# Cross-attention and quantised feed-forward: the opening in another order

## The chip, the cores and the metric

The kernel runs on one core of one Trainium2 chip. The metric is the device time of one execution in microseconds (us); the kernel before has a median of 1361.93 us over 3 runs (1360.26 to 1363.41). The engines are TensorE (PE, whose weight loads the profile counts apart as PEld), VectorE (DVE), ScalarE (ACT), GpSimd (POOL) and SyncE (SP), which here issues all the DMAs.

## The reference

The input `x` is 8 x 1024 rows of 512; the context has 8 x 64 rows of 512. There are 16 heads of 64.

```python
lat = layernorm(_layernorm(x), ln_l_w, ln_l_b); c = layernorm(ctx, ln_c_w, ln_c_b)
q = lat @ Wq;  k, v = split(c @ Wkv)
attn = softmax(clip(q @ k.T * 64**-0.5, -11, 11))        # per head
x = x + (attn @ v) @ Wo + bo
xq = fake_quant(_layernorm(x), clip_x)                   # one scale for the whole tensor
h = fake_quant(silu(xq @ wq8(w_gate).T) * (xq @ wq8(w_up).T), clip_down)
x = x + h @ wq8(w_down).T
```

## The kernel before, in words

The kernel has an opening (0 to 99.4 us), an attention part in 16 groups of 512 rows, and a feed-forward part. The change touches the opening alone.

The attention never forms the queries. For each batch entry the keys are folded with the query weights into a matrix M (tile `M`), so that the scores of a group are products of the normalised rows with M; the values are folded with the output weights in the same way (`value_fold`, `VW`). All of these products run as three float16 matmuls on high and low halves (`split_products`, L78 to L80). So every operand is made twice: ScalarE writes the high half, VectorE the low half (`weight_high` L492 and `weight_low` L713, `kv_high` L497 and `kv_low` L718, `q_high` L503 and `q_low` L722, `wo_high` L508 and `wo_low` L727, and for M `fold_key` L420 and L605).

The opening goes through these stages, each engine in the order in which its program is written:

1. Loads: context, vectors, then query weights (`wq32`, in the place of `x`), key weights (`wk32`, in the place of `M`), value weights (`wv32`, in the place of `E`), two groups of `x`. ScalarE sums the squares of each weight matrix (`square`, L485), from which its scale follows through a small matmul (`weight_sum` L1053 or `spread_rows` L1057) and a chain of small VectorE operations.
2. Key products: the first two together, chunk by chunk (`first_products`), then six more (`product(0, n)`, 12 matmuls each). Behind each, four transposes of query weights (`turn_q`, L1115).
3. Value products (`product(1, n)`, eight times 12 matmuls). Among them stand the folding of M (`fold_keys`, L991, 48 small matmuls for each quarter), the score bias (`project_bias` L1092, eight columns; `split_q_bias` L778 to L784; `bias_product` L1101, 24 matmuls; `bias_expand` L1107) and the first rows of group 0 (`norm_rows`, `high_y`, `low_y`, and the DMA transpose `turn`).
4. Step 0: eight tiles of scores of group 0 (`score`, tile `ring`), each followed on ScalarE by `cap` L445, `floor` L451 and `exp` L455, while the rows of group 1 are normalised; then `fold_values` (L1015), the denominators, and step 1.

An engine runs strictly in the order of its program. Engines meet by semaphores: PE starts a product only when `kv_low` has freed one of the two banks `po`, a quarter of the fold only when `m_lo` says that VectorE has taken the quarter before the last, and the first score when `m_lo` has reached 8. The identifiers `wk_lo`, `wv_lo`, `c_lo`, `squared2`, `m_lo` in the rows of the order are such semaphores.

## Time and profile before

| | us |
|---|---|
| median of 3 runs | 1361.93 |
| profiled execution | 1363.62 |
| its span in the trace | 1361.9 |
| PE busy (95% of the span) | 1289.0 |
| DVE busy | 1166.1 |
| ACT busy | 787.2 |

The span is what the trace covers; the profiled execution's own time is 1.7 us longer. All places are given in us from the start of the span. "Idle before" in a row of a timeline is the time in which the engine stood still just before, and the arrow names who released it. In the lines of the kernel before, the chain of waits is on PE for nearly all of the time.

### The profile page before, as it was taken

What the parts mean: (1) busy time and instruction counts of PE and PEld (TensorE: products, weight loads), DVE (VectorE), ACT (ScalarE), POOL (GpSimd) and SP (SyncE); (2) the same over time, 40 slices, a digit from 0 to 9 for tenths busy, and PEclk for the clock granted to TensorE, in tenths of its full rate; (3) what the DMA queues carried; (4) which work ended last, traced back from release to release, by engine and by line L of the source; (5) the groups of instructions that cost most, each with busy time, mean ns of one, the idle gap of its engine ahead of it and who ended that gap; (6) DMA issues with size and microseconds to landing.
All of it is one profiled execution on the core that took longest, in us unless ns stands there. A gap on an engine that the chain in (4) does not pass through costs nothing.

```text
span 1361.9 us, 20412 instructions
## 1 busy us (share of the span) xinstructions
PE 1289.0 (95%) x7625; PEld 610.7 (45%) x7668; DVE 1166.1 (86%) x2059; ACT 787.2 (58%) x1183; POOL 409.0 (30%) x278
## 2 busy tenths in 40 slices
PE   7988999999999999999999999699999999799997
PEld 6433444544544445445444444344444444344343
DVE  6757899988988998889889857789999999789996
ACT  6557765776577557755764762233443443597671
POOL 2104424542454244424443521000000000045555
PEclk9998999999999999999999999899999999899999
DMA  7173525446246245362561335296666632299995
GB/s 286 43 220 105 128 81 158 135 124 202 74 127 216 64 148 163 109 205 59 155 219 54 115 125 131 101 284 218 204 253 254 252 104 63 93 391 423 424 400 189
DMA packets 179218, 241.72 MB, mean 177 GB/s; under 512 B 121632, under 2 KB 140848, under 8 KB 168112
## 3 DMA queue, kind: packets, MB, share of 16 engines
q1 hardware_dynamic: 179120, 240.43, 53.2%
q8 instruction: 60, 0.98, 0.3%
q14 instruction: 38, 0.31, 0.1%
HBM read 120.86 MB, written 90.57 MB: 155 GB/s over the span
## 4 chain that ended last, share of the span: by engine, by line
PE 71%; DVE 14%; ACT 5%; issue 4%; SPq 3%; DMA 2%; POOL 1%; POOLq 0%; DVEq 0%; ACTq 0%
PE pu L1482 10%; PE pg L1476 10%; PE pu L1510 7%; PE po L78 7%; PE po L80 7%; PE po L79 7%; PE ring L79 6%; PE ring L78 6%; PE ring L80 6%; DVE w L1448 2%; PE ring L1015 1%; ACT E L451 1%; DVE sg L1455 1%; PE ring L991 1%; SPq L1247 1%
## 5 line engine op out<-in xcount | busy, mean ns | idle before, releaser
L1351 ACT ACTIVATE sg<-pg,gate_scale 128x512 f32<-128x512 f32 x176 | 120.9, 687 | 186.9 <-PE pg L1476 186.9
L78 PE MATMUL ring<-yT,M 128*128 128x512 f16 x512 | 195.5, 382 | 0.0
L80 PE MATMUL ring<-yT,M 128*128 128x512 f16 x512 | 195.4, 382 | 0.0
L79 PE MATMUL ring<-yT,M 128*128 128x512 f16 x512 | 195.4, 382 | 0.0
L78 PE MATMUL po<-VW,p 128*128 128x512 f16 x480 | 182.8, 381 | 2.0 <-DVE p L633 2.0
L1476 PE MATMUL pg<-xqT,w 128*128 128x512 bf16 x689 | 179.5, 380 | 3.7 <-DMA xqT<-xq 2.0
L80 PE MATMUL po<-VW,p 128*128 128x512 f16 x480 | 182.7, 381 | 0.0
L79 PE MATMUL po<-VW,p 128*128 128x512 f16 x480 | 182.5, 380 | 0.0
L1482 PE MATMUL pu<-xqT,w 128*128 128x512 bf16 x690 | 179.7, 380 | 0.7
L1510 PE MATMUL pu<-w 128*128 128x512 bf16 x690 | 157.4, 386 | 19.6 <-DVE w L1450 10.1
L392 POOL TENSOR_TENSOR esum<-esum,E 128x512 f32<-128x512 f32 x96 | 131.0, 1365 | 76.3 <-ACT E L455 76.2
L633 DVE TENSOR_TENSOR p<-E,p 128x512 f16<-128x512 f32 x120 | 143.9, 1200 | 6.5 <-ACT p L466 6.5
L466 ACT ACTIVATE p<-E 128x512 f16<-128x512 f32 x120 | 75.0, 625 | 126.4 <-DVE E L629 124.3
L1410 DVE TENSOR_TENSOR hb<-pu,sg 128x512 f32<-128x512 f32 x176 | 120.5, 685 | 30.9 <-PE pu L1482 29.4
L1368 ACT ACTIVATE hb<-hb,magic,hscale 128x512 f32<-128x512 f32 x176 | 125.2, 801 | 31.0 <-DMA hb<-hidden 27.2
L1414 DVE TENSOR_REDUCE hmax_g<-hb 128x1 f32<-128x512 f32 x176 | 117.4, 674 | 0.0
L1510 PEld LDWEIGHTS pu<-w 128*128 128x128 bf16 x704 | 68.4, 99 | 108.3 <-DVE sg L1455 14.5
L383 POOL TENSOR_TENSOR x<-x,bo 128x512 f32<-128x512 f32 x64 | 100.5, 1571 | 33.1 <-DVE y L597 33.1
L601 DVE TENSOR_TENSOR y<-y 128x512 f16<-128x512 f32 x64 | 56.3, 879 | 61.9 <-ACT y L416 61.8
L1476 PEld LDWEIGHTS pg<-xqT,w 128*128 128x128 bf16 x704 | 68.9, 98 | 86.8 <-DMA xqT<-xq 2.5
L1482 PEld LDWEIGHTS pu<-xqT,w 128*128 128x128 bf16 x704 | 69.1, 98 | 83.7 <-issue 1.1
L1336 POOL PARTITION_ALL_REDUCE one<-one x2 | 0.7, 350 | 348.2 <-DVE one L1435 316.8
(239 smaller groups left out, 2152.4 us busy)
## 6 DMA issues: line engine op xcount, KB each, us to landing
hidden<-hb SPq DMA_DIRECT2D x11, 2816.0 KB, 9.7
hb<-hidden SPq DMA_DIRECT2D x11, 2816.0 KB, 18.4
xa<-x_rows_d SPq DMA_DIRECT2D x28, 1024.0 KB, 6.1
x<-in_x_dram SPq DMA_DIRECT2D x16, 1024.0 KB, 5.8
value_fold<-E SPq DMA_DIRECT2D x64, 256.0 KB, 2.5
VW<-value_fold SPq DMA_DIRECT2D x16, 1024.0 KB, 6.1
x_rows_d<-x SPq DMA_DIRECT2D x16, 1024.0 KB, 4.9
out_dram<-xa SPq DMA_DIRECT2D x12, 1024.0 KB, 12.7
```

The lines of the kernel that those rows point to most:

```text
L78: nc.tensor.matmul(out, a_hi, b_hi, start=first, stop=False)
L79: nc.tensor.matmul(out, a_hi, b_lo, start=False, stop=False)
L80: return nc.tensor.matmul(out, a_lo, b_hi, start=False, stop=last)
L392: nc.gpsimd.tensor_tensor(esum[:], esum[:], E[:, g % 2, t], ALU.add).then_inc(sums, 1)
L633: nc.vector.tensor_tensor(probs(g, 1, t), E[:, g % 2, t], probs(g, 0, t), ALU.subtract).then_inc(prob_lo, 1)
L1351: nc.scalar.activation(sg[:, n % 4], pg[n % 4][:], ACT.Silu, scale=gate_scale[:, n % FT:n % FT + 1]).then_inc(silus, 1)
L1368: nc.scalar.activation(hb[:, slot, m], hb[:, slot, m], ACT.Identity, scale=hscale[:, m:m + 1], bias=magic[:, 0:1]).then_inc(h_scaled, 1)
L1410: nc.vector.tensor_tensor(hb[:, HOME[g], i], pu[n % 4][:], sg[:, n % 4], ALU.mult).then_inc(hs, 1)
L1414: nc.vector.tensor_reduce(hmax_g[:, i:i + 1], hb[:, HOME[g], i], AX.X, ALU.max, apply_absolute_value=True).then_inc(reaches, 1)
L1476: ins = nc.tensor.matmul(pg[n % 4][:], wg[:, c, at], xqT[:, g % 2, c], start=(c == 0), stop=(c == DC - 1))
L1482: ins = nc.tensor.matmul(pu[n % 4][:], wu[:, c, at], xqT[:, g % 2, c], start=(c == 0), stop=(c == DC - 1))
L1510: ins = nc.tensor.matmul(pu[t][:], hq[:, q % 2, m, t * P:(t + 1) * P], wd[:, m], start=(m == 0), stop=(m == FT - 1))
```

## The change

The loads of the opening come in the order keys, queries, values. The output weights are loaded into the place of `M` instead of `E`, as soon as the key weights have been converted. The four transposing DMAs of group 0 are issued ahead of the store of the keys. The eight `project_bias` columns leave the stretch before the key products and stand behind `product(0, 2)` to `product(0, 7)` and behind the first two value products. The squares of two chunks of query weights and of the value weights are taken later. The folding of M is done in one piece in front of the last value product. The output weights get their halves beside value products 3 to 6, where `norm_stats(1)` stands as well, and the score bias is finished at value product 4.

```diff
@@ -128,7 +128,8 @@
     wide = lambda half: half.rearrange("p (c n) -> p c n", c=DC)
     wk32 = wide(M[:, :, :, :, :].rearrange("p a c t u -> p (a c t u)").bitcast(fp32))
     wq32 = wide(x[:, 2:4].rearrange("p g t d -> p (g t d)"))
-    wv32, wo32 = wide(E[:, 1].rearrange("p t n -> p (t n)")), E[:, 1]
+    wv32 = wide(E[:, 1].rearrange("p t n -> p (t n)"))
+    wo32 = M[:, :, :, :, :].rearrange("p a c t u -> p (a c t u)").bitcast(fp32).rearrange("p (k n) -> p k n", k=IC)
     halves16 = lambda flat: flat.rearrange("p (a c n) -> p a c n", a=2, c=DC)
     parts16 = lambda flat: flat.rearrange("p (b a c s) -> p b a c s", b=NB, a=2, c=IC)
     vw_flat = VW[:, :, :, :].rearrange("p a t n -> p (a t n)")
@@ -256,9 +257,9 @@
             wkv_of = wkv.rearrange("(c p) (k n) -> k p c n", p=P, k=2)
             wq_of = wq.rearrange("(c p) n -> p c n", p=P)
             for c in range(DC):
+                sp.dma_start(wk32[:, c], wkv_of[0][:, c]).then_inc(ld_w[0][c], 16)
+            for c in range(DC):
                 sp.dma_start(wq32[:, c], wq_of[:, c]).then_inc(ld_w[1][c], 16)
-            for c in range(DC):
-                sp.dma_start(wk32[:, c], wkv_of[0][:, c]).then_inc(ld_w[0][c], 16)
             for c in range(DC):
                 sp.dma_start(wv32[:, c], wkv_of[1][:, c]).then_inc(ld_w[2][c], 16)
             load_x(0)
@@ -319,13 +320,14 @@
             sp.dma_start(x1_d[g], x[:, g % 4]).then_inc(x1_stored[g % 4], 16)
 
         load_opening()
-        sp.wait_ge(w_lo[1], DC)
+        sp.wait_ge(w_lo[0], DC)
         for c in range(DC):
             sp.dma_start(wo32[:, 2 * c:2 * c + 2], wo.rearrange("(c p) n -> p c n", p=P)[:, 2 * c:2 * c + 2]).then_inc(ld_w[3][c], 16)
-        store_kv(0)
         for t in range(TT):
             turn(0, t)
+        store_kv(0)
         sp.wait_ge(q_lo, IC)
+        sp.wait_ge(qb_ready, 1)
         for g in range(2, 4):
             load_x(g)
         sp.wait_ge(kv_stored, 16)
@@ -417,6 +419,8 @@
 
         def fold_key(b, u):
             act.wait_ge(m_psum, 8 * b + u + 1)
+            if b == 0 and u == 0:
+                act.wait_ge(o_lo, DC)
             nc.scalar.activation(M2[:, 0, u // 2, :, u % 2, :], ring[u % 4][:].rearrange("p (t u) -> p t u", t=KT),
                                  ACT.Copy, scale=mcol[:, u // 2:u // 2 + 1]).then_inc(m_hi, 1)
 
@@ -510,41 +514,44 @@
         act.wait_ge(magic_set, 2)
         nc.scalar.activation(warm[:], magic[:, 0:1], ACT.Identity)
         for c in range(DC):
+            square(0, wk32[:, c], c)
+        for c in range(2):
             square(1, wq32[:, c], c)
-        for c in range(DC):
-            square(0, wk32[:, c], c)
         act.wait_ge(scales, 1)
         for c in range(DC):
             act.wait_ge(c_turned, c + 1)
             nc.scalar.activation(cT[:, 0, c, :], ring[c][:], ACT.Identity, scale=ccol[:, 0, c:c + 1], bias=ccol[:, 1, c:c + 1]).then_inc(c_hi, 1)
             nc.scalar.activation(cf[:, c], ring[c][:], ACT.Identity, scale=ccol[:, 0, c:c + 1], bias=ccol[:, 1, c:c + 1]).then_inc(c_full, 1)
-            if c > 0:
-                weight_high(0, c - 1)
-        weight_high(0, DC - 1)
-        square(2, wv32[:, 0], 0)
+            weight_high(0, c)
         kv_high(0, 0)
         kv_high(0, 1)
-        for n in range(IC):
-            if n >= 2:
-                kv_high(0, n)
+        square(1, wq32[:, 2], 2)
+        square(1, wq32[:, 3], 3)
+        square(2, wv32[:, 0], 0)
+        for n in range(2, IC):
+            kv_high(0, n)
+            q_high(n - 2)
+            if n < 5:
+                square(2, wv32[:, n - 1], n - 1)
+            if n >= 6:
+                weight_high(1, n - 6)
+        for n in range(6, IC):
             q_high(n)
-            if n < 3:
-                square(2, wv32[:, n + 1], n + 1)
-            if n >= 4:
-                weight_high(1, n - 4)
+            weight_high(1, n - 4)
         act.wait_ge(ld_misc, 48)
         nc.scalar.activation(keep.clips[:], keep.clips[:], ACT.Exp, scale=-1.0).then_inc(sig, 1)
         for n in range(IC):
+            if n == IC - 1:
+                for u in range(KT):
+                    fold_key(0, u)
             kv_high(1, n)
             if n < 4:
-                fold_key(0, 2 * n)
-                fold_key(0, 2 * n + 1)
                 high_y(0, n)
-            if n in (3, 4):
-                for c in range(2 * n - 6, 2 * n - 4):
+            if n < 2:
+                for c in range(2 * n, 2 * n + 2):
                     square(3, wo32[:, 2 * c:2 * c + 2].rearrange("p k n -> p (k n)"), c)
-        for k in range(DC):
-            wo_high(k)
+            if 3 <= n < 7:
+                wo_high(n - 3)
 
         for s in range(NG):
             more = s + 1 < NG
@@ -814,54 +821,59 @@
         context_centre()
         vectors_known()
         scale_by_sum(WK, po[1][:, 0:DC], 1, 2)
-        rows_seen(WQ, 0)
         for c in range(DC):
             dve.wait_ge(c_full, c + 1)
             nc.vector.tensor_tensor(cT[:, 1, c, :], cf[:, c], cT[:, 0, c, :], ALU.subtract).then_inc(c_lo, 1)
-            if c > 0:
-                weight_low(0, c - 1)
-        weight_low(0, DC - 1)
-        scale_by_rows(WQ, misc[:, 0:P], 2, 3)
-        norm_stats(0)
+            weight_low(0, c)
         kv_low(0, 0)
         kv_low(0, 1)
+        rows_seen(WQ, 0)
+        norm_stats(0)
+        kv_low(0, 2)
+        scale_by_rows(WQ, misc[:, 0:P], 2, 3)
         q_low(0)
-        q_low(1)
-        for n in range(2, IC):
+        for n in range(3, IC):
             kv_low(0, n)
+            q_low(n - 2)
+            if n == 3:
+                norm_aggregates(0)
+            if n == 4:
+                norm_rstd(0)
+            if n == 5:
+                scale_by_sum(WV, misc[:, 0:DC], 2, 4)
+            if n >= 6:
+                weight_low(1, n - 6)
+        for n in range(6, IC):
             q_low(n)
-            if n == 2:
-                norm_aggregates(0)
-                norm_rstd(0)
-            if n == 3:
-                scale_by_sum(WV, misc[:, 0:DC], 2, 4)
-            if n >= 4:
-                weight_low(1, n - 4)
+            weight_low(1, n - 4)
         norm_rows(0, 0)
         norm_rows(0, 1)
-        split_q_bias()
         score_scales()
         for n in range(IC):
+            if n == IC - 1:
+                for u in range(KT):
+                    fold_key(0, u)
             kv_low(1, n)
             if n < 4:
-                fold_key(0, 2 * n)
-                fold_key(0, 2 * n + 1)
                 low_y(0, n)
                 if n < 2:
                     norm_rows(0, n + 2)
-            if n == 5:
+            if n == 1:
+                split_q_bias()
                 rows_seen(WO, 1)
-            if n == 6:
+            if n == 2:
                 scale_by_rows(WO, pd[:, 0:P], 3, 5)
-            if n == 7:
+            if n == 3:
                 dve.wait_ge(bias_rows, 1)
                 nc.vector.tensor_copy(bias_rows_sb, misc[0:H, :]).then_inc(rows_out, 1)
-        score_biases()
-        norm_stats(1)
+            if n == 4:
+                score_biases()
+            if 3 <= n < 7:
+                wo_low(n - 3)
+            if n == 6:
+                norm_stats(1)
         norm_aggregates(1)
         norm_rstd(1)
-        for k in range(DC):
-            wo_low(k)
 
         for s in range(NG):
             more = s + 1 < NG
@@ -1071,8 +1083,6 @@
                     ins = product_chunk(0, n, c)
                     if c == DC - 1:
                         ins.then_inc(kv_ready[0], 1)
-                if c < 2:
-                    project_bias(6 + c)
 
         def product(kind, n):
 
@@ -1120,10 +1130,6 @@
         pe.wait_ge(ld_vec, 64)
         nc.tensor.transpose(misc[:, 0:4 * DC], vec_rows, keep.ident32[0:4 * DC, 0:4 * DC]).then_inc(const_turned, 1)
         spread_vectors()
-        for c in range(DC):
-            pe.wait_ge(ld_w[1][c], 16)
-        project_bias(0)
-        project_bias(1)
         for t in range(TT):
             pe.wait_ge(c_centred, t + 1)
             for c in range(DC):
@@ -1131,28 +1137,35 @@
                 if t == TT - 1:
                     ins.then_inc(c_turned, 1)
         weight_sum(0, po[1][:, 0:DC])
-        project_bias(2)
-        spread_rows(0, misc[:, 0:P], 2)
-        for n in range(3, 6):
-            project_bias(n)
         first_products()
+        for c in range(DC):
+            pe.wait_ge(ld_w[1][c], 16)
         turn_q(0)
         turn_q(1)
         for n in range(2, IC):
             product(0, n)
+            if n == 2:
+                spread_rows(0, misc[:, 0:P], 2)
             turn_q(n)
-            if n == 3:
+            project_bias(n - 2)
+            if n == 4:
                 pe.wait_ge(scales, 3)
                 weight_sum(2, misc[:, 0:DC])
         for n in range(IC):
+            if n == IC - 1:
+                for c in range(DC):
+                    fold_keys(0, c)
             product(1, n)
-            if n < 4:
-                fold_keys(0, n)
-            if n == 6:
+            if n < 2:
+                project_bias(n + 6)
+            if n == 2:
                 pe.wait_ge(qb_split, 2)
                 spread_rows(1, pd[:, 0:P], 3)
+            if n == 3:
+                pe.wait_ge(scales, 4)
                 bias_product()
-        bias_expand()
+            if n == 4:
+                bias_expand()
 
         for s in range(NG):
             more = s + 1 < NG
```

Three places show what moves. The first is PE from the end of the context's transposes (`weight_sum`, into `po`) to the second chunk of the first key products. Before:

```order
L1053 MATMUL po<-weight_squares,ones_row 128x4 [waits squared0]
L1092 MATMUL pd<-vector_cols,x 128x1 x4
L1057 MATMUL misc<-ffn_raw,ones_row 128x128 [waits spread_in]
L1092 MATMUL pd<-vector_cols,x 128x1 x12
L78 MATMUL po<-cT,VW 128x512 [waits wk_lo,wk_hi,c_lo]
L79 MATMUL po<-cT,VW 128x512
L80 MATMUL po<-cT,VW 128x512
L78 MATMUL po<-cT,VW 128x512
```

and after the change:

```order
L1065 MATMUL po<-weight_squares,ones_row 128x4 [waits squared0]
L78 MATMUL po<-cT,VW 128x512 [waits wk_lo,wk_hi,c_lo]
L79 MATMUL po<-cT,VW 128x512
L80 MATMUL po<-cT,VW 128x512
L78 MATMUL po<-cT,VW 128x512
L79 MATMUL po<-cT,VW 128x512
```

The sixteen `project_bias` matmuls of these rows (into `pd`) and the spread of the query weights' scale that stood in front are gone; of the eight columns none is left here.

The second is ACT at the end of the key products: L497 and L501 are `kv_high`, L503 and L507 `q_high`, L492 and L496 `weight_high` of the value weights. Before, from `product(0, 6)` on:

```order
L497 ACTIVATE p<-po 128x8x64 [waits k_ready]
L503 ACTIVATE w<-ring,operand_scales 128x512 [waits q_turned]
L492 ACTIVATE E<-E,operand_scales 128x1024
L497 ACTIVATE p<-po 128x8x64 [waits k_ready]
L503 ACTIVATE w<-ring,operand_scales 128x512 [waits q_turned]
L492 ACTIVATE E<-E,operand_scales 128x1024
L536 ACTIVATE clips<-clips 128x2 [waits ld_misc]
```

and after the change, from `product(0, 7)` on:

```order
L501 ACTIVATE p<-po 128x8x64 [waits k_ready]
L507 ACTIVATE w<-ring,operand_scales 128x512 [waits q_turned]
L496 ACTIVATE E<-E,operand_scales 128x1024
L507 ACTIVATE w<-ring,operand_scales 128x512 [waits q_turned]
L496 ACTIVATE E<-E,operand_scales 128x1024
L507 ACTIVATE w<-ring,operand_scales 128x512 [waits q_turned]
L496 ACTIVATE E<-E,operand_scales 128x1024
L542 ACTIVATE clips<-clips 128x2 [waits ld_misc]
```

Behind the last key product one query piece and one value chunk stood before; now there are three query pieces and three value chunks.

The third is DVE at the folding of M (L605 and L612 are the low halves of `fold_key`). Before, with the rows of group 0 (`y`) between them:

```order
L718 TENSOR_TENSOR VW<-po,VW 128x8x64 [waits v_hi16,open_step]
L605 SCALAR_TENSOR_TENSOR M<-ring,key_cols,M 128x8x64 [waits m_hi] x2
L601 TENSOR_TENSOR y<-y 128x512 [waits y_hi]
L597 TENSOR_SCALAR y<-x,mv,rs 128x512 [waits y_lo]
L718 TENSOR_TENSOR VW<-po,VW 128x8x64 [waits v_hi16]
L605 SCALAR_TENSOR_TENSOR M<-ring,key_cols,M 128x8x64 [waits m_hi] x2
```

and after the change, where L734 is `wo_low`, L585 `norm_stats(1)` and L725 `kv_low`:

```order
L725 TENSOR_TENSOR VW<-po,VW 128x8x64 [waits v_hi16]
L734 SCALAR_TENSOR_TENSOR w<-M,operand_scales,w 128x1024 [waits wo_hi]
L585 BN_STATS st<-x 128x6 [waits x_loaded1]
L585 BN_STATS st<-x 128x6 x3
L612 SCALAR_TENSOR_TENSOR M<-ring,key_cols,M 128x8x64 [waits m_hi] x8
L725 TENSOR_TENSOR VW<-po,VW 128x8x64 [waits v_hi16]
L591 BN_AGGR mv<-st 128x2 [waits ln_step] x4
```

The eight low halves of M now stand in one row, behind the last piece of output weights and the statistics of group 1.

## Rows read from the trace of the kernel before

**Rows 1.** Page, busy time of the engines over the span

```profile
PE 1289.0 (95%) x7625; PEld 610.7 (45%) x7668; DVE 1166.1 (86%) x2059; ACT 787.2 (58%) x1183; POOL 409.0 (30%) x278
```

**Rows 2.** Timeline of PE: start, us, engine, line, xcount [idle before <-releaser]

```profile
22.17 5.12 PE L1092 MATMUL pd<-vector_cols,x 128*128 128x1 f32 x24
...
39.73 1.04 PE L1115 MATMUL ring<-ident,x 128*128 128x128 f32 x8
...
58.54 0.60 PE L1115 MATMUL ring<-ident,x 128*128 128x128 f32 x4
...
62.41 0.38 PE L78 MATMUL po<-yT,E 128*128 128x512 f16 x1 [3.27 <-DVE E L713]
```

**Rows 3.** Timeline of PE, value products to the first score

```profile
66.78 0.87 PE L991 MATMUL ring<-p,w 64*128 64x64 f16 x48
...
88.26 5.35 PE L1101 MATMUL misc<-p,ffn_raw 128*16 128x512 f16 x24
...
98.37 1.12 PE L1107 MATMUL misc<-rexp,head_rows 16*128 16x512 f32 x2 [2.07 <-DVE rexp L858]
...
99.43 0.39 PE L78 MATMUL ring<-yT,M 128*128 128x512 f16 x1
```

**Rows 4.** Timeline of ACT and PE in step 0

```profile
100.53 0.63 PE L80 MATMUL ring<-yT,M 128*128 128x512 f16 x1
...
111.87 0.63 ACT L416 ACTIVATE y<-y 128x512 f16<-128x512 f32 x1 [3.83 <-DVE y L597]
...
127.58 0.71 ACT L455 ACTIVATE E<-E,score_bounds 128x512 f32<-128x512 f32 x1
...
134.57 0.59 PE L78 MATMUL ring<-yT,M 128*128 128x512 f16 x1
```

**Rows 5.** Chain of waits, start, us, what: single matmuls and one turn

```profile
32.67 0.43 PE po L78
...
43.43 0.44 PE ring L1115 x4
...
44.51 0.22 PE po L78
```

**Rows 6.** Timeline up to the first key products, DVE, ACT and POOL

```profile
17.93 0.23 DVE L754 TENSOR_SCALAR context_cols<-vector_cols,operand_scales 128x8 f32<-128x8 f32 x1
...
19.04 0.78 ACT L519 ACTIVATE cT<-ring,context_cols 128x512 f16<-128x512 f32 x1 [0.36 <-PE ring L1130]
...
26.43 2.21 ACT L492 ACTIVATE VW<-M,operand_scales 128x1024 f16<-128x1024 f32 x2
...
27.36 10.18 POOL L397 COPY yT<-cT 128x512 f16<-128x512 f16 x8 [24.43 <-DVE cT L820]
...
27.64 3.88 DVE L713 SCALAR_TENSOR_TENSOR VW<-M,operand_scales,VW 128x1024 f16<-128x1024 f32 x2 [0.35 <-ACT VW L492]
```

**Rows 7.** Timeline of ACT and DVE, end of the key products

```profile
44.71 1.07 ACT L485 ACTIVATE E<-E 128x1024 f16<-128x1024 f32 x1
...
58.74 0.60 ACT L497 ACTIVATE p<-po 128x512 f16<-128x512 f32 x1 [0.82 <-PE po L80]
...
60.98 1.28 DVE L713 SCALAR_TENSOR_TENSOR E<-E,operand_scales 128x1024 f16<-128x1024 f32 x1 [0.26 <-ACT E L492]
```

**Rows 8.** Timeline of ACT and DVE: operations that the change moves

```profile
63.09 0.21 DVE L778 TENSOR_SCALAR scale_tmp<-operand_scales 128x1 f32<-128x1 f32 x1
...
66.04 0.16 DVE L788 TENSOR_TENSOR scale_tmp<-operand_scales 128x1 f32<-128x1 f32 x1
...
74.69 1.26 ACT L420 ACTIVATE M<-ring,key_cols 128x512 f16<-128x512 f32 x2 [0.21 <-PE ring L991]
...
75.41 1.41 DVE L605 SCALAR_TENSOR_TENSOR M<-ring,key_cols,M 128x512 f16<-128x512 f32 x2 [0.20 <-ACT M L420]
...
101.15 2.47 DVE L578 BATCH_NORM_STATS2 st<-x 128x6 f32<-128x512 f32 x4
...
106.51 4.87 DVE L727 SCALAR_TENSOR_TENSOR w<-E,operand_scales,w 128x1024 f16<-128x1024 f32 x4
```

## Prediction

> **What bounds the kernel now.** I read the page first, for the share of TensorE: it is busy 1289.0 of 1361.9 us [rows 1], so what the change can move is time in which PE stands still or runs slowly. The change touches the opening alone, so I then read the waits of PE up to 140 us, the chain of waits there, and the timelines of the three engines. The reader is to see four stretches, each ending with an instruction of PE that exists before and after:
>
> A: start to the end of the first pair of key products, 39.73 us.
> B: from there to the first value product, 62.41: 22.68 us. It ends with a wait of 3.27 us for the last low half of the value weights [rows 2].
> C: to the first score, 99.43: 37.02 us. Its last wait is 2.07 us in front of `bias_expand` [rows 3].
> D: step 0, to the first score of step 1, 134.57: 35.14 us [rows 3, 4].
>
> What follows is the same work in the same order, so I let any shift at 134.57 stand in the total.
>
> In A PE runs at half rate: matmuls of 512 columns follow each other by 0.43 us, against 0.22 later; that is 1.2 and 2.4 GHz [rows 5].
>
> **Stretch A: earlier.** Before, twelve `project_bias` matmuls (three columns) hold PE from 22.17 for 5.12 us, so the first key product starts behind them, though its operands are there sooner; two more columns stand between the chunks. All leave. What is late next is the conversion of the key weights. ScalarE starts it at 19.04, when PE has turned the context; VectorE has the scales 18.16 (17.93 + 0.23). With no columns ahead of it, PE turns the context earlier, and with keys loaded first the squares of the keys are done earlier too, so ScalarE starts at about 18.2, 0.8 sooner. Its last high half then ends at 27.8 instead of 28.6 (26.43 + 2.21), and the low half follows at 29.2 to 30.1: the last two took 3.88 us beside GpSimd's copies, 1.94 each, against 1.28 for one alone [rows 6, 7]. Six matmuls remain behind it: 1.3 us at the high level, 2.6 at the low. I take 31.9 (30.5 to 33): A gains 7.8 us, 6.7 to 9.2.
>
> The Trainium skill, "SBUF — State Buffer", section "SBUF: two separate sides", says that VectorE with two SBUF inputs and a GpSimd operation reading SBUF exclude each other for a whole instruction. GpSimd's eight copies took 10.18 us [rows 6], so by that rule the last low half could wait one copy, 1.27, and end at 30.5 instead of 29.9; the trace's 1.94 lies between. By that rule A would gain 0.5 us less.
>
> **Stretch B: longer.** Before, PE needs 18.81 us from 39.73 to the end of `product(0, 7)` at 58.54 [rows 2]. Now comes on top:
> - Five of the eight columns in front of that point. A column costs 5.12 / 3 = 1.7 at the low level. The trace shows none at the high level; the ends are 0 (it hides under other loads) and 1.7. I take half, 0.85, as for the matmuls of [rows 5]: 4.2 us.
> - The spread of the query scale, 0.4, and a wait of about 0.5 for it: ScalarE now squares two chunks of query weights and one of value weights behind `kv_high(0, 1)`, at 1.07 and a read of the sum each [rows 7].
> - `weight_sum(2)` behind `product(0, 4)`. The last square of the value weights now stands behind `kv_high(0, 4)` and `q_high(2)`: 0.6 + 0.6 + 1.2 = 2.4, and ScalarE is a further 1 us behind from the squares before it; PE has 0.44 (four transposes) + 0.85 of other work [rows 5]. Wait 2.0 (0.5 to 2.5). Before, that square came one product earlier and cost nothing.
>
> So 25.9 us to the end of `product(0, 7)`. The first value product then waits for ScalarE, whose row is now one `kv_high`, three `q_high` and three `weight_high` (one, one and one before): 0.60 + 3 x (0.6 + 1.1) = 5.7, and a last low half, 1.28, with 0.1 of hand-over: 7.1 us instead of 3.87 (58.54 to 62.41) [rows 2, 7]. B takes 33.0 us, 10.3 more; ends 30 and 35.
>
> **Stretch C: longer.** Up to the end of value product 6: 84 matmuls at 0.22, 18.5; `bias_product` 5.35; `bias_expand` 1.12, its rows now copied in time; two columns 1.7; the spread of the output scale 0.4 [rows 3, 5]. New is a wait in front of that spread: the last column ends the second product's slot, then VectorE does `kv_low`, `low_y`, `norm_rows` and `split_q_bias` (63.09 to 66.04, 2.95 us) and `rows_seen`, while PE has one product of 2.6: 2.3 us (0 to 3). And the low clock after the wait of 7 us: after 3.27 us of idling it showed low matmuls too; I count 2.5 us (1 to 3.4). Sum 31.9 us.
>
> Then the fold. PE does two quarters and needs VectorE's low halves of the first before the third. On VectorE stand ahead of them `kv_low` 0.6, the last `wo_low` 1.2 and `norm_stats(1)` 2.47; with ScalarE's `kv_high` 0.6 and `wo_high` 1.05 in front of `wo_low`, they start 5.4 us after value product 6. Eight low halves at 0.68 (1.41 for a pair, overlapped) follow, broken by the alternation with PE and ScalarE (0.87 for a quarter, 1.26 for two high halves) [rows 3, 8]. M's first half is free at 5.4 + 1.4 = 6.8, the third quarter ends at 7.7, the fourth at 8.5 to 9.3, and the last value product at 11.7. Before, the quarters stood between products and PE did not wait for them. I add 1.0 for the clock after a wait of 5 us. C: 31.9 + 11.7 + 1.0 = 44.6, 7.6 more; ends 39 and 48. The DMAs that move (output weights earlier, transposes ahead of the store) only end waits of ScalarE that PE never felt; the output weights are asked for 30 us before they are squared, and the first conversion of M waits for `wo_low` at 3 us, inside the 5.4.
>
> **Stretch D: shorter.** Before, the 4.87 us of `wo_low`, the statistics of group 1 and its scale chain stand on VectorE behind the first score; ScalarE waits 3.83 us for rows until 111.87. Now only the scale chain, about 2.8 us, remains, and it runs beside the first tile. The pace is then PE's, 96 matmuls at 0.22 = 21.1, plus 1.5 for the low level (it fell at 100.53 before), then cap, floor, rows and exp of the last tile, 2.8, and from the end of exp (127.58 + 0.71) to step 1 as before, 6.3: 31.7 us, 3.4 less; ends 26 and 33 [rows 4, 8].
>
> **Sum.** -7.8 + 10.3 + 7.6 - 3.4 = +6.7 us on the profiled execution of 1363.62 (span 1361.9 and 1.7 around it): 1370.3. That execution lies 1.7 above the median of 1361.93; the forecast for the median is 1368.6, rounded to 1368.
>
> **Rivals.**
> 1. *Step 0 becomes PE's and the clock holds (faster).* If ScalarE's tile of about 2.4 us stays under PE's 2.6 and the fold of the values runs through, step 0 is 21.1 + 3 for the folds + 1.8 for the denominators = 25.9, 9.2 less instead of 3.4. With the 3.5 us of low clock counted in C gone too: 6.7 - 5.8 - 3.5 = -2.6, and with the wait for the last squares at its low end, -4.1: 1357.8. For it: ScalarE waited for rows in step 0 and no longer does. Against: the 6.3 us behind the last exp are a chain of exp, fold and denominators that the change doesn't touch. It decides from a step 0 under 27 us.
> 2. *The added waits are half as long (no change).* If a column costs little at the high level and VectorE comes to the fold 3 us earlier, B and C lose 6 us less: +0.7, 1362.6. For it: columns were never measured at the high level. Against: the row of seven ScalarE instructions has measured prices.
> 3. *The low level follows each new wait.* The waits of 2 us at `weight_sum(2)` and of 2.3 us at the spread each bring slow matmuls, as the 2.07 us wait did, behind which matmuls took 0.63 from 100.53 on [rows 3, 4]. A stretch like A's shows the price, 0.21 a matmul; 8 to 12 of them at each place: +4, 1372.6. The Trainium skill, "TensorE: Matmul & The Clock Gate", section "HAM oscillation — how this bites in real kernels", says that every wait that makes the array idle long enough starts the next matmuls slowly again. The trace agrees behind 98.37; by that rule this rival is what happens.
>
> **Chances.** Forecast 0.45 (own range 1365 to 1371), rival 3 0.18, rival 2 0.2, rival 1 0.17. A measurement of this kernel can tell about 0.2%, 2.7 us, from no change. Faster 0.17, within it 0.21 and slower 0.62. The range that should hold the time 8 times in 10: from just under rival 2 toward rival 1, 1359, to rival 3 with its long ends, 1374.
>
> **What would show it.** In the changed kernel's timeline: first pair done near 32; a wait of PE for `weight_sum(2)` of 1 to 2 us; the wait in front of the first value product 5 us or more (3.27 before), ending near 65; a wait for `m_lo` of about 5 us inside the fold; first score near 109 (99.43 before); step 0 near 32 us. The forecast is wrong if the first score stands before 103, or if step 0 takes under 28 us, or if a wait in a later step grows or disappears.

## The result, and the profile after

The changed kernel takes 1367.02 us (median of 7 runs, 1363.39 to 1367.75), the kernel before 1361.47 in the same set (7 runs, 1360.26 to 1363.41): a ratio of 1.0036, with a 95% interval of 1.0024 to 1.0047. A second set, further down, gives 1.0029 (1.0016 to 1.0042). So it is slower by 0.3 to 0.4%: the medians differ by 5.5 us in the first set and by 2.4 in the second. Forecast were 1368.0, with 1359 to 1374 as the range.

The profiled execution of the changed kernel is the lowest of its seven, 1363.39 (span 1361.6); that of the kernel before, 1363.62, lies 2.2 above its median. The two profiles therefore end at nearly the same time, and have to be compared stretch by stretch. The page's first line, against [rows 1]:

```profile
PE 1279.1 (94%) x7668; PEld 602.3 (44%) x7668; DVE 1163.6 (85%) x2059; ACT 787.3 (58%) x1183; POOL 408.2 (30%) x278
```

PE is 9.9 us less busy, with the same work, though the span is the same: part of the work now runs at the high level, and the time went into waits. These are PE's waits up to 150 us (releaser: us in total, times, longest):

```profile
PE po L78 <- DVE E L720: 6.2, 1, 6.2
PE po L78 <- DVE VW L720: 5.8, 3, 3.9
PE ring L1003 <- DVE M L612: 5.2, 1, 5.2
...
PE pd L1069 <- DVE ffn_raw L709: 1.8, 1, 1.8
...
PE misc L1065 <- ACT E L489: 1.2, 1, 1.2
```

The first row is the wait in front of the first value product (3.27 in [rows 2]), the second are three waits for the halves of the key weights in A, the third is the one inside the fold. L1069 is the spread of the output scale and L1065 `weight_sum(2)`: these four (all but the second row) stand where the forecast put them. PE's timeline (start, us, engine, line, operation [idle before <-releaser]), against [rows 2 to 4]:

```profile
29.74 0.38 PE L78 MATMUL po<-cT,VW 128*128 128x512 f16 x1 [1.51 <-DVE VW L720]
31.03 1.04 PE L1125 MATMUL ring<-ident,x 128*128 128x128 f32 x8
...
35.62 0.95 PE L1102 MATMUL pd<-vector_cols,x 128*128 128x1 f32 x8
...
45.41 0.36 PE L1065 MATMUL misc<-weight_squares,ones_row 128*128 128x4 f32 x2 [1.17 <-ACT E L489]
...
57.57 0.60 PE L1125 MATMUL ring<-ident,x 128*128 128x128 f32 x4
...
65.15 0.58 PE L78 MATMUL po<-yT,E 128*128 128x512 f16 x1 [6.20 <-DVE E L720]
...
70.00 0.95 PE L1102 MATMUL pd<-vector_cols,x 128*128 128x1 f32 x8
...
96.10 1.57 PE L1003 MATMUL ring<-p,w 64*128 64x64 f16 x96
...
102.90 2.78 PE L1003 MATMUL ring<-p,w 64*128 64x64 f16 x96 [5.23 <-DVE M L612]
...
109.04 0.38 PE L78 MATMUL ring<-yT,M 128*128 128x512 f16 x1
...
138.55 0.38 PE L78 MATMUL ring<-yT,M 128*128 128x512 f16 x1
```

In the order of the stretches (us):

| | before | forecast | after | difference, forecast / measured |
|---|---|---|---|---|
| A, to the first pair | 39.73 | 31.9 | 31.03 | -7.8 / -8.7 |
| B, to the first value product | 22.68 | 33.0 | 34.12 | +10.3 / +11.4 |
| C, to the first score | 37.02 | 44.6 | 43.89 | +7.6 / +6.9 |
| D, step 0 | 35.14 | 31.7 | 29.51 | -3.4 / -5.6 |
| start of step 1 | 134.57 | 141.2 | 138.55 | +6.7 / +4.0 |

The row of A compares with an execution in which PE was slow for long. Experiments e2 and g2, further down, have the instructions of A as they were, and there A ended at 36.95 and 35.57, not at 39.73. So the change's own gain in A lies between 4.5 and 8.7 us, and 2.8 to 4.2 us of it can be the execution that was profiled.

The changed kernel is 4.0 us late at the start of step 1. By the end this is gone in the two profiles, and not through the change. Step 1's first matmuls ran slowly before and fast after, which takes 1.7; another 1.7 falls at 722 us, and 0.9 behind it. At 722 the kernel before shows this (PE's timeline):

```profile
721.60 0.50 PE L79 MATMUL po<-VW,p 128*128 128x512 f16 x1
721.89 0.63 PE L80 MATMUL po<-VW,p 128*128 128x512 f16 x1
722.32 0.63 PE L78 MATMUL po<-VW,p 128*128 128x512 f16 x1
...
725.23 0.38 PE L79 MATMUL po<-VW,p 128*128 128x512 f16 x1
```

and the changed one, at the same products, this:

```profile
723.67 0.38 PE L78 MATMUL po<-VW,p 128*128 128x512 f16 x1
723.89 0.38 PE L79 MATMUL po<-VW,p 128*128 128x512 f16 x1
```

Matmuls 0.43 apart in the one, 0.22 in the other, in code that the change doesn't touch. One more profile of the changed kernel has no slow matmuls there either, eight of the nine other kernels tried below have them in theirs, within 713 to 729 us. Why just these profiles lack them was not settled.

### The profile page after: what moved, and what is told of

Same layout as the page of the kernel before. It is cut to its first block, busy times and chain, and to the rows that moved or that the text cites. A ratio compares the mean times of both kernels' runs of the same rounds, so it can differ in the third digit from the quotient of the medians.

```text
span 1361.6 us, 20458 instructions
## 1 busy us (share of the span) xinstructions
PE 1279.1 (94%) x7668; PEld 602.3 (44%) x7668; DVE 1163.6 (85%) x2059; ACT 787.3 (58%) x1183; POOL 408.2 (30%) x278
## 4 chain that ended last, share of the span: by engine, by line
PE 72%; DVE 15%; ACT 5%; issue 3%; SPq 3%; DMA 1%; POOL 1%; POOLq 0%; DVEq 0%; ACTq 0%
PE pg L1489 10%; PE pu L1495 10%; PE pu L1523 8%; PE po L78 7%; PE po L79 7%; PE po L80 7%; PE ring L80 6%; PE ring L78 6%; PE ring L79 6%; DVE w L1461 2%; PE ring L1027 1%; PE ring L1003 1%; DVE sg L1468 1%; ACT E L455 1%; SPq L1260 1%
## 5 line engine op out<-in xcount | busy, mean ns | idle before, releaser
L1489 PEld LDWEIGHTS pg<-xqT,w 128*128 128x128 bf16 x704 | 68.6, 98 | 87.0 <-DMA xqT<-xq 3.8
```

The costliest lines, as they stand in the source:

```text
L1489: ins = nc.tensor.matmul(pg[n % 4][:], wg[:, c, at], xqT[:, g % 2, c], start=(c == 0), stop=(c == DC - 1))
```

## The experiments

Two explanations stood against each other for the loss. Mine: the squares and halves of the value weights now stand behind key work on ScalarE (B), the columns of the bias run where PE would have worked on, and the fold in a row waits for VectorE (C); step 0 gives some back. The rival: the loss is the low level of TensorE's clock behind each new wait. The four columns of places are read from each run's profile, at the same instructions as above. The ratio is formed from all runs of both kernels, and is not the quotient of two medians; the medians of the kernel before, taken beside each set, lie between 1361.12 and 1361.47.

| kernel | median (range, runs) us | ratio to before (95% interval) | A ends | first value product | first score | start of step 1 |
|---|---|---|---|---|---|---|
| before (profile) | | | 39.73 | 62.41 | 99.43 | 134.57 |
| after | 1367.02 (1363.39-1367.75, 7) | 1.0036 (1.0024-1.0047) | 31.03 | 65.15 | 109.04 | 138.55 |
| after, second set | 1363.80 (1361.66-1367.56, 12) | 1.0029 (1.0016-1.0042) | 30.98 | 63.42 | 107.52 | 137.03 |
| e1 first half | 1366.40 (1364.71-1370.60, 6) | 1.0041 (1.0026-1.0057) | 30.97 | 65.07 | 102.85 | 138.01 |
| e2 second half | 1358.48 (1355.51-1363.78, 12) | 0.9986 (0.9972-1.0000) | 36.95 | 59.62 | 100.44 | 130.33 |
| e3 statistics behind fold | 1367.78 (1362.52-1372.52, 7) | 1.0053 (1.0032-1.0073) | 31.11 | 63.54 | 106.33 | 136.35 |
| e4 squares in the gap | 1359.99 (1358.09-1364.82, 12) | 0.9996 (0.9984-1.0009) | 31.00 | 59.83 | 102.52 | 131.83 |
| f1 keep busy | 1363.37 (1359.77-1367.95, 12) | 1.0019 (1.0004-1.0034) | 31.04 | 65.14 | 105.34 | 135.24 |
| g1 columns in waits | 1354.07 (1351.52-1355.36, 9) | 0.9953 (0.9938-0.9968) | 31.21 | 56.36 | 94.46 | 124.57 |
| g2 second half, statistics | 1358.44 (1353.36-1361.97, 12) | 0.9985 (0.9972-0.9999) | 35.57 | 58.25 | 99.03 | 128.53 |
| h1 columns alone | 1359.42 (1354.49-1361.70, 12) | 0.9994 (0.9980-1.0009) | 32.46 | 57.94 | 93.58 | 128.74 |
| h2 last product inside | 1353.28 (1348.28-1353.67, 6) | 0.9943 (0.9928-0.9958) | 31.18 | 56.31 | 93.96 | 123.47 |

**e1: the first half alone** (keys first, columns behind the products, the new row of squares; the fold, output weights and statistics as before).

```diff
-            if n == IC - 1:
-                for c in range(DC):
-                    fold_keys(0, c)
             product(1, n)
+            if n < 4:
+                fold_keys(0, n)
...
```

> The part up to the first value product is that of the changed kernel (loads, bias columns, squares, value halves); from there on it is as before (output weights in E's place and loaded late, M folded in quarters between products, transposes behind the store), but for the last two bias columns, which stay behind the first two value products, and split_q_bias with them. My theory (every stretch moves the end by its own length): stretch B ends 2.7 us later than before (65.15 against 62.41), two columns add 1.9 and the slow matmuls behind the wait of 6 us about 1 more: 1366 to 1367, 4.5 to 5.5 us over before. Rival (the loss lies in the fold and its wait, the first part is neutral): within 1 us of before, 1361.5. Rival (chance of TensorE's low level only): runs spread over 4 us, median 1363.

Measured 1.0041, all of the change's loss. In the profile the wait of 6.2 us in front of the value products is there, and the one inside the fold is not; step 0 takes 35.2 us, as before.

**e2: the second half alone** (output weights in M's place, fold in a row, statistics; columns and loads as before), the same edit the other way round.

> The complement: up to the first value product as before; from there on as changed (output weights into M's place, transposes ahead of the store, M folded in one row ahead of the last value product, halves of the output weights and statistics beside products), without bias columns among the value products. My theory: the wait in the fold costs 5.2 and two shorter terms, the wait at bias_expand (2.07) goes, step 0 gives back 3.5 to 5.6: 1360 to 1364, my number 1362. Rival (the fold in a row is the whole loss): 1366 to 1367, as changed. The two halves together should give the change of the whole, 5.5 us.

Measured 0.9986, at the edge of faster, where I had expected no gain. With e1's 1.0041 the two halves add up to 1.0027, near the whole's 1.0029 and 1.0036. PE's waits in e2:

```profile
PE ring L999 <- DVE M L610: 5.2, 1, 5.2
...
PE po L78 <- DVE E L718: 3.3, 1, 3.3
...
PE pd L1065 <- DVE ffn_raw L707: 2.4, 1, 2.4
```

The fold's wait of 5.2 us is paid in full, but step 0 takes 29.9 us instead of 35.1. From the first value product to step 1 it is 70.7 us, for 72.2 before. The second half is not where the change loses. Its A ended at 36.95, 2.8 earlier than before with the same instructions: matmuls follow each other by 0.43 us up to 33.1 us there, and up to 39.1 in the profile of before.

**e3: statistics behind the fold**, which frees VectorE 2.5 us earlier for the fold.

```diff
-            if n == 6:
-                norm_stats(1)
+        norm_stats(1)
```

> The changed kernel with norm_stats(1) moved from in front of the eight low halves of M to behind the last value product (VectorE, 2.46 us). My theory: the wait of PE for m_lo inside the fold shrinks from 5.2 to about 2.8 us and the first score comes 2.3 us sooner; the statistics then run beside the first tile, where VectorE has slack: 1364.7, 2.3 us under the changed kernel. Rival (what limits the fold is ScalarE, which waits for wo_low): the wait stays near 5 us and the time within 0.5 us of the changed kernel. Rival (the statistics were free there and are not free in step 0): slower by up to 2 us.

The wait shrank by less than the 2.46 us taken away, and the median isn't lower. PE's wait:

```profile
PE ring L1002 <- DVE M L612: 3.8, 1, 3.8
```

The first score stands at 106.33, 1.2 to 2.7 us earlier than in the two profiles of the changed kernel; of that, C itself gives 1.1 to 1.3 us (42.8 for 43.9 and 44.1), and the rest is where C began. The 2.3 us that I expected didn't come. Its runs reach from 1362.5 to 1372.5, so the effect on the time can't be read. g2, the same edit on e2, has e2's time within 0.1 us.

**e4: the squares in the gap** that ScalarE has before the first pair of key products: two squares of query weights ahead of that pair's `kv_high`, three of value weights right behind it, the fourth two products earlier than in the changed kernel, and the high halves one place earlier. The low halves on VectorE, the spread of the query scale and `weight_sum(2)` move forward with them; the cut shows ScalarE's part.

```diff
-        kv_high(0, 0)
-        kv_high(0, 1)
         square(1, wq32[:, 2], 2)
         square(1, wq32[:, 3], 3)
-        square(2, wv32[:, 0], 0)
-        for n in range(2, IC):
+        kv_high(0, 0)
+        kv_high(0, 1)
+        for c in range(3):
+            square(2, wv32[:, c], c)
+        kv_high(0, 2)
+        q_high(0)
+        q_high(1)
+        square(2, wv32[:, 3], 3)
+        for n in range(3, IC):
             kv_high(0, n)
-            q_high(n - 2)
-            if n < 5:
-                square(2, wv32[:, n - 1], n - 1)
-            if n >= 6:
-                weight_high(1, n - 6)
+            q_high(n - 1)
+            if n >= 5:
+                weight_high(1, n - 5)
...
```

> The changed kernel with ScalarE's squares taken early: those of the query weights in its idle time ahead of the first key products (2.9 us of waiting there), those of the value weights right behind, so that the value halves start one product sooner and only one query piece and one value chunk stand behind the last key product; the spread of the query scale ahead of product 2, and weight_sum(2) one product earlier. My theory: the wait of 1.2 us at weight_sum(2) goes, that in front of the first value product falls from 6.2 to 3 or 4 us: 1362 to 1363.5, 4 us under the changed kernel. Rival (the wait there is set by VectorE's row of q_low and weight_low and not by ScalarE): less than 1 us. Rival (clock): the same time, with a wider spread of runs.

Measured 1359.99: 3.8 to 7.0 us under the changed kernel. PE's wait in front of the first value product:

```profile
PE po L78 <- DVE E L722: 4.3, 1, 4.3
```

The wait for `weight_sum(2)` is gone. The first value product starts 3.6 to 5.3 us earlier. The whole loss is gone, so this order, in which the squares and halves of the value weights stand behind key work, is the largest part of it. ScalarE's row and VectorE's were moved together, so their shares are not separated.

**The changed kernel once more**, beside the runs of f1, g1 and g2:

> The changed kernel itself, on the chip of this call, as the base for the others, whose runs spread over 4 to 10 us: 1366 to 1368 by its own seven runs. If its profile shows the slow stretches at 721 us that the first profile of it lacks, its end lies about 2.5 us later for the same first score.

Measured 1363.80, under the 1366 to 1368 that I expected. The sign stands, and the size is less certain than one set's interval says: 3.2 us lie between two sets of the same kernel.

**f1: PE kept busy in the two long waits**, by 26 and 21 matmuls whose result nobody reads.

```diff
+        pe.wait_ge(scales, 4)
+        keep_busy(26)
...
+                    if c == 2:
+                        pe.wait_ge(biases, 1)
+                        keep_busy(21)
```

> The changed kernel with matmuls of 128x512 f16 added whose result nobody reads: 26 in PE's wait in front of the first value product (6.2 us) and 21 in its wait inside the fold (5.2 us), each shorter than the wait it stands in. My theory (besides its length, each wait costs the slow matmuls behind it: 12 at 4.85 us instead of 2.6 behind the first, 4 to 8 behind the second): 3 us less than the changed kernel on the same chip, 1363 to 1364.5. Rival (the low level costs nothing that the waits for VectorE don't hide): the same time as the changed kernel. Rival (the added matmuls delay the products): slower by 1 us or more.

PE's timeline in f1, where the changed kernel's matmuls from 65.15 took 0.63 each:

```profile
58.80 5.77 PE L1121 MATMUL misc<-cT 128*128 128x512 f16 x26
65.14 0.38 PE L78 MATMUL po<-yT,E 128*128 128x512 f16 x1 [0.57 <-DVE E L720]
65.35 0.38 PE L79 MATMUL po<-yT,E 128*128 128x512 f16 x1
```

and the windows of PE (us, busy time and count of each engine, PEclk the granted clock, DMA share, GB/s), of the changed kernel

```profile
58.00:65.00 7.00, 0.96 (x10) 0.87 (x8) 6.34 (x8) 5.30 (x8) 0.00 (x0) 0.85 0.00 0
65.20:69.80 4.60, 4.60 (x12) 1.54 (x13) 3.48 (x6) 0.00 (x0) 2.65 (x2) 0.50 0.02 4
```

and of f1

```profile
58.00:65.00 7.00, 6.57 (x36) 3.25 (x34) 6.35 (x8) 5.28 (x8) 0.00 (x0) 1.00 0.01 2
65.00:70.00 5.00, 4.86 (x27) 2.78 (x28) 4.86 (x8) 2.08 (x5) 2.65 (x2) 1.00 0.00 0
```

So in this place the idle stretch brings the low level, and filling it keeps the high one. C takes 40.2 us, for 43.9 and 44.1 in the changed kernel, and the first score comes 2.2 to 3.7 us earlier. Of that, and of the 3 us that I expected at the end, the median shows 0.4 against the second set of the changed kernel (1363.37 and 1363.80), which is no measurable gain: f1 runs slowly at the start of step 1 (135.2 to 138.8) and from 722 to 726 in its profile, where the changed kernel did not. The low level behind the two long waits costs 3.7 to 3.9 us in C; whether that is worth anything at the end stays open.

**g1: the columns where PE waits anyway** (e4, and: two columns and a third in front of or between the first key products, where PE waits for the key weights, the other five in front of the value products; `split_q_bias` ahead of them, the spread of the output scale one product later, and the statistics behind the fold).

```diff
+        project_bias(0)
+        project_bias(1)
         first_products()
         ...
+        for n in range(3, IC):
+            project_bias(n)
         for n in range(IC):
-            if n < 2:
-                project_bias(n + 6)
...
```

> e4 (squares early) with the eight bias columns in PE's waits: two ahead of the first key product, one ahead of its last chunk, five in the wait in front of the first value product; split_q_bias ahead of the value products; the spread of the output scale one product later; norm_stats(1) behind the fold. My theory (what limits is the sum of PE's row and its waits): seven columns at 0.95, 1.8 for the spread's wait and about 2 in the fold leave PE's row: 1351 to 1354, 7 us under e4 and 9 under before. Rival (ScalarE and VectorE take over as the bound of the key products): at most 3 us under e4, 1357.

Measured 1354.07, faster than both kernels, and at the upper end of my 1351 to 1354. Of the waits for the value weights and for the two sums nothing above 0.2 us is left; among PE's waits up to 140 us are:

```profile
PE ring L1002 <- DVE M L614: 3.8, 1, 3.8
...
PE po L78 <- DVE VW L722: 0.5, 1, 0.5
```

**g2: e2 with the statistics behind the fold.**

> The second half of the change alone (e2) with norm_stats(1) behind the fold. Theory (the statistics cost the fold 1.4 to 2.4 us): 1356.5, 2 us under e2. Rival (as e3 beside the changed kernel, which came out no faster in its median): the same as e2, 1358.5, because what the fold gains the clock or step 0 takes back.

1358.44 against e2's 1358.48: moving the statistics is worth nothing that can be measured, and the 2 us that I expected didn't come.

**h1: the columns alone.** The kernel before, with the columns placed as in g1; its loads and order otherwise.

> The kernel before with one thing of the change done alone: the bias columns leave the stretch ahead of the key products. Two stay there, in PE's wait for the key weights, one stands ahead of the last chunk, five in the wait in front of the first value product; loads, squares, halves, fold and statistics as before. My theory (gain of stretch A without the price of B): the first pair of key products ends 7 us earlier, the five columns fill the wait of 3.27 and add 1.5: first value product 5 us earlier, 1356 to 1358. Rival (the gain of A is lost again in the key products, whatever the rest does, as in the changed kernel): 1361. Rival (A's gain needs the keys loaded first): first pair only 3 us earlier, 1359.

Its A ends at 32.46 without keys loaded first, and the start of step 1 is 5.8 us earlier in the profile, but the ratio is 0.9994 (0.9980 to 1.0009). My 1356 to 1358 was too low. Part of A's gain is thus the columns', not the order of the loads; how much of it reaches the end was not settled. What g1 has beyond h1 stands in step 0, where g1 takes 30.1 us and h1 35.2: that is what the second half gave e2 as well.

**h2: the last value product inside the fold**, between its second and third quarter, on g1; its halves move with it on ScalarE and VectorE.

```diff
-                for c in range(DC):
-                    fold_keys(0, c)
+                fold_keys(0, 0)
+                fold_keys(0, 1)
             product(1, n)
+            if n == IC - 1:
+                fold_keys(0, 2)
+                fold_keys(0, 3)
```

> g1 with the last value product between the second and the third quarter of the fold, so that it fills PE's wait for m_lo (3.8 us), and its halves between those of the fold. My theory: the wait before the third quarter falls from 3.8 to about 1.2 us, but a wait for the last low halves of M, of about 1 to 1.5 us, opens ahead of the first score, where the last product covered it: 1352.5, 1.5 us under g1. Rival (VectorE's row of eight low halves sets the first score either way): no difference.

PE's waits there:

```profile
PE ring L78 <- DVE M L617: 2.6, 1, 2.6
...
PE ring L1008 <- DVE M L617: 1.5, 2, 1.1
```

The wait of 3.8 us shrank to 1.5 (in two parts) and a new one of 2.6 stands in front of the first score: VectorE's low halves set the end of the fold, wherever PE waits for them. 1353.28, the lowest of all medians, is 0.8 us under g1, which their runs don't tell apart.

## Why the prediction was right

**A, -7.8 forecast, -8.7 measured.** The changed kernel's last pair of halves (DVE's timeline):

```profile
25.35 1.28 DVE L720 SCALAR_TENSOR_TENSOR VW<-M,operand_scales,VW 128x1024 f16<-128x1024 f32 x1 [0.34 <-ACT VW L496]
...
27.72 1.88 DVE L720 SCALAR_TENSOR_TENSOR VW<-M,operand_scales,VW 128x1024 f16<-128x1024 f32 x1 [0.34 <-ACT VW L496]
```

The last ends at 29.60 (29.2 to 30.1 forecast), and the six matmuls behind it took 1.29 us, at the high level; I had taken a value between the two levels. Beside GpSimd's eight copies (from 27.44, 9.36 us) the half took 0.60 more than alone. The Trainium skill, "SBUF — State Buffer", section "SBUF: two separate sides", has the two exclude each other for a whole instruction; by that the half could have lost up to a copy, 1.17. The measurement, about half a copy, lies within that, as it did before [rows 6]; it doesn't tell the rule from another one. The end of A was worked out from the rows of the conversion, and holds. As a gain over the kernel before, -7.8 hangs on one slow execution's 39.73: against the 36.95 and 35.57 of e2 and g2 A gained 5.9 and 4.5.

**B, +10.3 and +11.4.** To the end of `product(0, 7)` 26.5 us (25.9 forecast). A column costs 0.81 to 0.95 at the high level, where I had taken 0.85 as a middle. The wait for `weight_sum(2)` was 1.17 instead of 2.0, and behind it came what rival 3 said: slow matmuls from 45.8 to 49.4, some 1.7 us. So the first part of B is right by two errors of opposite sign (0.8 too much wait, 1.7 of low level that was not counted), and that is luck. From there to the first value product 7.6 (7.1 forecast): ScalarE's row was as priced, and the rest is a low half of the query weights, 0.74, which stands on VectorE ahead of the last one of the value weights (DVE's timeline):

```profile
63.07 0.74 DVE L729 SCALAR_TENSOR_TENSOR w<-ring,operand_scales,w 128x512 f16<-128x512 f32 x1
63.73 1.27 DVE L720 SCALAR_TENSOR_TENSOR E<-E,operand_scales 128x1024 f16<-128x1024 f32 x1
```

**C, +7.6 and +6.9.** 30.95 us to the end of value product 6 (31.9 forecast), with the spread's wait 1.85 for 2.3 and 2.3 us of low level for 2.5. The fold's third quarter starts 6.80 us behind it, where the forecast had M's first half free at 6.8. VectorE's row there was as read from the order:

```profile
97.87 1.28 DVE L734 SCALAR_TENSOR_TENSOR w<-M,operand_scales,w 128x1024 f16<-128x1024 f32 x1 [0.35 <-ACT w L512]
99.08 2.46 DVE L585 BATCH_NORM_STATS2 st<-x 128x6 f32<-128x512 f32 x4
101.46 2.71 DVE L612 SCALAR_TENSOR_TENSOR M<-ring,key_cols,M 128x512 f16<-128x512 f32 x4
```

The first score is 12.9 us behind the end of value product 6, for 12.7.

**D, -3.4 and -5.6.** ScalarE waits for no rows any more, and the tiles follow each other by 2.59 us, PE's pace. The last tile's `cap` and exp (ACT's timeline):

```profile
129.96 0.78 ACT L449 ACTIVATE E<-ring,score_bias,score_scale 128x512 f32<-128x512 f32 x1 [0.30 <-PE ring L80]
...
131.92 0.71 ACT L459 ACTIVATE E<-E,score_bounds 128x512 f32<-128x512 f32 x1
```

It is 23.6 us to the end of this exp, for 25.4. The 1.5 us of low level that I had counted there, because the kernel before showed it from 100.5 to 104.1, did not come. The tail behind the exp took 5.9, for 6.3. Rival 1's 25.9 wasn't reached for two reasons: its sum left out the last tile's chain on ScalarE, 2.7 us here, and had 4.8 for the tail.

**The sum** to the start of step 1 was 2.7 us too high (+6.7 for +4.0), and 2.2 of that are D, the term that was mis-sized. The median was forecast too high as well: 1368.0 for 1367.02 and 1363.80, of which the second lies outside my own 1365 to 1371. That any shift there stands in the total holds only in the mean: from the start of step 1 to the end, where the change touches nothing, the profiles took 1227.3 us (before), 1223.05 and 1222.9 (after), and 1223 to 1230 over all kernels. The medians differ by 2.4 to 5.5, around the 4.0.

**The rivals.** Rival 1 (step 0 becomes PE's): the first half of it happened, the step's tail stayed. Rival 2 (waits half as long): fell, the waits of 6.2 and 5.2 were full. Rival 3 (low level behind each wait): true behind `weight_sum(2)` in one of the two profiles and behind both long waits in both, not behind the spread's 1.85 (matmuls 0.22 apart from 79.11 on). Behind a wait of 3.27 us the kernel before fell (matmuls 0.43 apart from 63.15 on), and e2 and g2 with the same wait did not. The Trainium skill, "TensorE: Matmul & The Clock Gate", section "HAM oscillation — how this bites in real kernels", says that a wait that is long enough makes the next matmuls start slowly. The changed kernel and f1 agree with that at the wait of 6.2 us (0.50 behind it, 1.00 where it is filled); the falls without any wait, below, are not covered by it. As for my theory, e1, e2 and e4 bear it out for the first half; I had also counted the fold in a row as a loss, and e2 shows that what step 0 gives back makes up for it (its ratio of 0.9986 reaches 1.0000).

## What to carry to other kernels

Work without a reader nearby, as the bias columns here, belongs where the engine waits for another one anyway: g1, with the columns there, is 5.9 us under e4, which has them behind the products. (`split_q_bias` and the spread were moved with them and not tried alone; the statistics, moved too, were worth nothing in g2.) An earlier first product is worth only what the engines behind it do with the time: A ended 8.7 us earlier in the profile, with the columns moved and the keys loaded first, and B took all of it back, because the columns now stood between the key products and the next weights' squares behind key work on ScalarE. And a shift at one place in a profile is to be compared with the median only after asking which stretches ran at the low level in just that execution.

## What the runs showed of the hardware

In the first part of a trace the granted clock's rows can't be relied on. The kernel before, windows as above:

```profile
27.00:39.00 12.00, 12.00 (x39) 6.68 (x39) 7.63 (x13) 2.68 (x4) 10.18 (x8) 1.00 0.04 9
...
134.60:138.10 3.50, 3.50 (x10) 1.29 (x11) 3.09 (x17) 3.22 (x2) 0.00 (x0) 0.51 0.76 263
```

In both stretches matmuls follow each other by 0.43 us, yet the first reads 1.00. In the changed kernel the matmuls from 22.0 to 25.4 read 0.50 at the same pace. So what the prediction said of A's half rate rests on the matmuls' spacing, which the clock's row doesn't confirm there.

PE can fall without a wait. In g1 it is busy throughout from 50 us on, from 51.1 with the five columns (single-column matmuls); the clock falls while they run, and the value products behind them start at the low level:

```profile
50.00:56.00 6.00, 6.00 (x47) 5.69 (x45) 5.58 (x6) 3.92 (x6) 0.00 (x0) 0.87 0.01 3
54.40:56.30 1.90, 1.90 (x11) 1.90 (x10) 1.90 (x3) 0.33 (x2) 0.00 (x0) 0.51 0.00 0
56.30:61.10 4.80, 4.80 (x13) 1.77 (x14) 4.22 (x12) 0.00 (x0) 2.64 (x2) 0.50 0.00 0
```

h1 fell in the same place, without a wait, at 58.2 us, just behind its five columns. And PE can keep the high level over a wait of 3.27 us, as in e2 (the value product's row, and the window behind it):

```profile
59.62 0.38 PE L78 MATMUL po<-yT,E 128*128 128x512 f16 x1 [3.27 <-DVE E L718]
...
59.60:64.60 5.00, 4.98 (x24) 2.27 (x24) 4.66 (x13) 2.19 (x5) 2.65 (x2) 1.00 0.00 0
```

Where the slow stretches lie moves from one execution to the next, of one kernel too: the changed one ran slowly from 65.2 to 70.0 in one profile and from 63.4 to 68.6 in the other, and it had slow matmuls behind the wait for `weight_sum(2)`, from 45.8 to 49.4, in the first alone. The first value product starts 1.7 us later there, as much as some of the edits tried here.
